# Expert rows rounded and split on VectorE before their transpose, which runs in the rounded format

## What is computed

```python
logits = jnp.einsum('th,eh->te', xf, gate_w)
expert_idx = jnp.argmax(logits, axis=-1)
onehot = jax.nn.one_hot(expert_idx, gate_w.shape[0], dtype=x.dtype)
g = jnp.einsum('th,ehd->etd', xf, wg)
u = jnp.einsum('th,ehd->etd', xf, wu)
inter = jnp.square(jax.nn.relu(g)) * u
inter = inter * onehot.T[:, :, None]
out = jnp.einsum('etd,edh->th', inter, wd)
...
g = _silu(_L0_ffn_ref(xn, ...))
x = x + s * g
```

## Time and profile before

| | us |
|---|---|
| median of 3 runs | 510.59 |
| lowest and highest | 508.68 and 511.1 |
| the profiled execution's own time | 510.11 |
| its span, first to last instruction | 508.2 |
| PE busy | 494.7 (97%) |
| DVE busy | 452.9 (89%) |
| ACT busy | 395.6 (78%) |
| POOL busy | 319.8 (63%) |

### The profile page before, as it was taken

One profiled execution on the slowest core, in us unless ns is written; L12 is line 12 of the kernel. 1 busy time (PEld: TensorE's weight loads), 2 busy tenths in 40 slices (PEclk: granted clock), 3 DMA queues, 4 the chain that ended last, 5 costly groups with the idle time before them and its releaser, 6 DMA issues.

```text
span 508.2 us, 11940 instructions
## 1 busy us (share of the span) xinstructions
PE 494.7 (97%) x3599; PEld 462.8 (91%) x3599; DVE 452.9 (89%) x1428; ACT 395.6 (78%) x910; POOL 319.8 (63%) x377
## 2 busy tenths in 40 slices
PE   6899999999999999999999999999999999999996
PEld 5899999999999999889999997898888888888885
DVE  6899999999999988969889948999999999999985
ACT  4878878787878784378988865888888888888885
POOL 5568876767676777454552027777887777877300
PEclk9999999999999999999999999999999999999999
DMA  7942322222222114457878563265665565665411
GB/s 224 254 115 94 113 86 94 85 84 84 84 84 84 43 52 142 175 159 245 249 242 261 184 199 113 74 144 130 137 151 126 129 140 126 144 142 127 103 43 64
DMA packets 59303, 67.70 MB, mean 133 GB/s; under 512 B 11880, under 2 KB 53616, under 8 KB 59248
## 3 DMA queue, kind: packets, MB, share of 16 engines
q1 hardware_dynamic: 44304, 38.69, 25.1%
q0 software_dynamic: 14944, 28.32, 22.3%
HBM read 39.85 MB, written 27.13 MB: 132 GB/s over the span
## 4 chain that ended last, share of the span: by engine, by line
PE 93%; DVE 3%; ACT 1%; issue 1%; DMA 1%; SPq 0%; DVEq 0%
PE q_ps L1524 11%; PE v_ps L1546 11%; PE gu_ps L1181 6%; PE s_ps L1566 6%; PE y_ps L1200 4%; PE k_ps L171 3%; PE m_ps L173 3%; PE m_ps L171 3%; PE k_ps L173 3%; PE m_ps L172 3%; PE k_ps L172 3%; PE t_ps L1157 3%; PE tq_ps L171 3%; PE tq_ps L172 3%; PE t_ps L1537 3%; PE tq_ps L173 3%
## 5 line engine op out<-in xcount | busy, mean ns | idle before, releaser
L1970 POOL DMA_INDIRECT four<-expert_rows,gather_u x64 | 68.5, 1071 | 37.2 <-DMA expert_rows<-y 18.5
L976 POOL DMA_INDIRECT sorted_rows<-xn,row_u x64 | 67.6, 1057 | 17.5 <-issue 14.3
L965 POOL TENSOR_TENSOR xn<-xn 128x512 fp32r<-128x512 f32 x32 | 43.2, 1350 | 30.5 <-ACT xn L581 30.4
L1524 PE MATMUL q_ps<-xt,wqk 128*128 128x256 f32 x256 | 60.6, 379 | 0.2 <-issue 0.2
L1546 PE MATMUL v_ps<-wvo,xt 128*128 128x256 f32 x248 | 58.7, 379 | 0.0
L1524 PEld LDWEIGHTS q_ps<-xt,wqk 128*128 128x128 f32 x256 | 48.5, 190 | 7.2 <-issue 0.7
L1546 PEld LDWEIGHTS v_ps<-wvo,xt 128*128 128x128 f32 x248 | 44.8, 190 | 4.8
L1976 POOL DMA_DIRECT2D res<-in_L_attn_x x26 | 34.9, 1341 | 18.7 <-DVE res L1773 17.1
L227 POOL DMA_DIRECT2D four<-sorted_rows x36 | 20.0, 555 | 39.9 <-PE t_ps L1157 35.0
L1985 POOL TENSOR_TENSOR rstd<-var_eps,neg_half 128x4 f32<-128x4 f32 x32 | 35.6, 1113 | 8.8 <-DVE var_eps L1809 8.7
L171 PE MATMUL tq_ps<-xt,wq 128*128 128x256 f32 x128 | 38.4, 300 | 1.7 <-DVE xt L715 1.7
(11 more groups left out here) (292 smaller groups left out, 1792.7 us busy)
## 6 DMA issues: line engine op xcount, KB each, us to landing
expert_rows<-y SPq DMA_DIRECT2D x35, 256.0 KB, 3.5
four<-in_L_attn_x SPq DMA_DIRECT2D x32, 256.0 KB
out_rows<-att SPq DMA_DIRECT2D x31, 256.0 KB
res<-in_L_attn_x POOLq DMA_DIRECT2D x26, 256.0 KB
four<-sorted_rows POOLq DMA_DIRECT2D x36, 128.0 KB, 3.4
four<-sorted_rows SPq DMA_DIRECT2D x36, 128.0 KB, 3.7
wdn<-in_L_ffn_wd SPq DMA_DIRECT2D x2, 512.0 KB, 7.2
sorted_rows<-res SPq DMA_DIRECT2D x8, 128.0 KB, 5.6
```

Of the source, the lines that this page charges most:

```text
L965: nc.gpsimd.tensor_tensor(xn2[:, s, 1], xn[:, i], xn2[:, s, 0].bitcast(F32), ALU.subtract).then_inc(g["xn_split"], 1)
L976: nc.gpsimd.indirect_dma_start(out=z.sorted_dram.ap(), out_offset=bass.IndirectOffsetOnAxis(ap=row_u[:, i // CU, k:k + 1], axis=0), in_=xn ...
L1524: m = nc.tensor.matmul(q_ps[:, j, :], wqk[:, k, j * P:(j + 1) * P], xt[:, i % 2, k, :], start=(j == 0 and k == 0), stop=(k == KD - 1), ski ...
L1970: nc.gpsimd.indirect_dma_start(out=moe[:, n % SLOTS, t, :], out_offset=None, in_=z.expert_dram.ap()[0:(z.SLOTS - 1) * P, :], in_offset=bas ...
```

## The change

`hidden` writes the product once, into a `hid` of 64 columns a tile, all in SBUF. Two new instructions on DVE follow in the same function: a copy of `hid` into the first half of `hid2` in the rounded format, and the difference `hid - rounded` into its second half. `turn_hidden` transposes `hid2` in fp32r, with an identity matrix in the same format (`ident_r`), which one new copy makes at the start of DVE's part of the stage. `copy_hidden` stays and now signals `ht_copied` itself; `hidden_rest` is gone. `gate_up` waits for the new semaphore `hid_made`, counted by the product, where it waited for `hid_ready`, now counted by the difference. The larger buffers move the space that the second layer keeps free from 3648 to 4032 numbers.

```diff
-        hid = sb("hid", [P, 2, 2, 2, DE])
+        hid = sb("hid", [P, 2, 2, DE])
+        hid2 = sb("hid2", [P, 2, 2, 2, DE], F32R)
+        ident_r = sb("ident_r", [P, P], F32R)
...
                 if reused:
-                    pe.wait_ge(g["hid_ready"], n - 1)
+                    pe.wait_ge(g["hid_made"], n - 1)
...
             def turn_hidden(n, i, reused):
+                if n == 0:
+                    pe.wait_ge(g["ident_rounded"], 1)
                 pe.wait_ge(g["hid_ready"], n + 1)
                 if reused:
                     pe.wait_ge(g["ht_copied"], n - 1)
                 for u in range(width(n)):
-                    t = nc.tensor.transpose(ht_ps[:, i % 2, u * P:(u + 1) * P], hid[:, i % 2, u].rearrange("p c f -> p (c f)"), z.ident[:])
+                    t = nc.tensor.transpose(ht_ps[:, i % 2, u * P:(u + 1) * P].bitcast(F32R), hid2[:, i % 2, u].rearrange("p c f -> p (c f)"), ident_r[:])
                 t.then_inc(g["ht_ready"], 1)
...
-                nc.scalar.activation(hidt[:, i % 2, 0:w], ht_ps[:, i % 2, 0:w * P].rearrange("p (u t) -> p u t", u=w), ACT.Copy).then_inc(g["ht_rounded"], 1)
+                nc.scalar.activation(hidt[:, i % 2, 0:w], ht_ps[:, i % 2, 0:w * P].rearrange("p (u t) -> p u t", u=w), ACT.Copy).then_inc(g["ht_copied"], 1)
...
-                twice = [P, w, 2, DE]
-                nc.vector.tensor_tensor(hid[:, i % 2, 0:w], o[:, :, DE:2 * DE].unsqueeze(2).to_broadcast(twice),
-                                        gate[:, i % 2, 0:w].unsqueeze(2).to_broadcast(twice), ALU.mult).then_inc(g["hid_ready"], 1)
-
-            def hidden_rest(n, i):
-                dve.wait_ge(g["ht_rounded"], n + 1)
-                w = width(n)
-                nc.vector.tensor_tensor(hidt[DE:P, i % 2, 0:w], ht_ps[DE:P, i % 2, 0:w * P].rearrange("p (u t) -> p u t", u=w),
-                                        hidt[DE:P, i % 2, 0:w], ALU.subtract).then_inc(g["ht_copied"], 1)
+                nc.vector.tensor_tensor(hid[:, i % 2, 0:w], o[:, :, DE:2 * DE], gate[:, i % 2, 0:w], ALU.mult).then_inc(g["hid_made"], 1)
+                dve.wait_ge(g["hid_made"], n + 1)
+                nc.vector.tensor_copy(hid2[:, i % 2, 0:w, 0], hid[:, i % 2, 0:w]).then_inc(g["hid_rounded"], 1)
+                dve.wait_ge(g["hid_rounded"], n + 1)
+                nc.vector.tensor_tensor(hid2[:, i % 2, 0:w, 1], hid[:, i % 2, 0:w], hid2[:, i % 2, 0:w, 0].bitcast(F32), ALU.subtract).then_inc(g["hid_ready"], 1)
...
-                if 1 <= m <= PAIRS:
-                    hidden_rest(m - 1, (m - 1) % QUAD)
...
+            nc.vector.tensor_copy(ident_r[:], z.ident[:]).then_inc(g["ident_rounded"], 1)
             divisors(START[0])
...
-    MOE_SPACE = 3648
+    MOE_SPACE = 4032
```

More of the change, by code:

```diff
@@ L1079, in experts @@
         y_banks = y_ps[:].rearrange("p i u d -> p i (u d)")
-        g = sems("weights_loaded shifts_ready shift_found t_ready t_copied gu_ready gate_relu squared hid_ready ht_ready ht_rounded ht_copied y_ready "
+        g = sems("weights_loaded shifts_ready shift_found t_ready t_copied gu_ready gate_relu squared hid_made hid_rounded hid_ready ht_ready ht_copied ident_rounded y_ready "
                  "y_tanh silu_ready wdn_rounded wdn_split w2_centred")
```

## The result

The changed kernel takes 515.87 us in the median of 4 runs (514.44 to 517.07), the kernel before 510.11 us beside it (4 runs, 508.68 to 511.1). The ratio is 1.0124, with an interval of 1.0103 to 1.0145: 1.2% slower. Forecast were 514.0 us and a range to 515.8. The direction was right, the loss was 5.8 us where 3.4 were expected, and the time lies just above the range.

What follows compares the result with a forecast made beforehand. PE, busy 97% of the span, was taken as the bound. Weights +2.9, split_end +1.2, removed waits -0.7 and transposes 0 gave +3.4 us on 510.11, or 513.5; with 0.5 for the median, 514.0 us, range 509.8 to 515.8.

Steps and rivals of the forecast that it cites:

- What bounds, and the chain: Expert steps: PE sets the pace at 2.03 us a step; DVE's new work of 1.77 us costs an undisturbed step nothing.
- What goes: PE's `down` no longer waits for `hidden_rest` where DVE was late, including the last steps: a gain of 0.7 us.
- -0.4: The sum in us that the forecast would end near without the rule that DVE and GpSimd share SBUF ports.
- DVE and GpSimd in SBUF: The new copy and difference, all operands in SBUF, stand still beside GpSimd's eleven operations: +2.9 and +1.2 us.
- turns: Rival at pair 1: SBUF access alternates between DVE and GpSimd, PE loads 1.6 us later, total 512.6 us; chance 22 in 100.
- no holding up: Rival: operations of 128 numbers are too short for the port lock to matter, 510.2 us, no change; chance 13 in 100.
- +2.9: Pair 1: three weight subtractions in a row hold the copy, PE loads 3.0 us later, less 0.1 of an old wait.
- split_end: Eight GpSimd operations, each starting with a step; four delay PE's load by 0.3 us each, +1.2 us in sum.
- the very first: The first of GpSimd's eight split_end operations, claimed to end when the copy comes, so given no cost.
- The transposes: 71 transposes of hidden rows change format to fp32r, claimed to stay at 0.11 us each: +0 us.
- Dear: Rival: the fp32r transposes of hidden rows take 0.22 us each, +7.8 us, total 521.8 us; chance 10 in 100.
- cheap transposes: Rival: the fp32r transposes of hidden rows take 0.06 us each, -3.5 us; chance 8 in 100, 2 more without holding up.

Runs made afterwards that it cites:

- e2: Changed kernel with GpSimd's three weight subtractions and eight split_end operations all held until behind DVE's copy and difference; 511.5 us, ratio 1.0007.
- e7: Changed kernel with the product written to PSUM and read there by copy and difference, GpSimd's operations left in place; 512.04 us, ratio 1.003.
- e6: Changed kernel with the rounded half written by a second product reading PSUM instead of the copy from SBUF; 515.84 us, ratio 1.0103.
- e3: Changed kernel with 25 unused identity transposes keeping PE busy ahead of the transpose of pair 1; 515.97 us, ratio 1.0101.
- e5: Kernel before the change, with DVE waiting ahead of pair 1's product until GpSimd's three weight subtractions end; 514.85 us, ratio 1.0084.
- e8: Changed kernel with only the eight split_end operations held behind the copy, the weight subtractions left at pair 1; 515.23 us, ratio 1.0096.
- e11: Kernel before the change, with the wait of e5 and the 25 unused transposes of e3; 512.37 us, ratio 1.0062.
- e1: Changed kernel with GpSimd's three weight subtractions moved apart, behind loads for pairs 8 to 10 and held until the difference; 514.34 us, ratio 1.005.
- e4: Changed kernel with its transposes of hidden rows in float32 again; 517.42 us, ratio 1.0113.
- e10: Kernel before the change, with the wait of e5 cut to two of GpSimd's three subtractions; 510.79 us, ratio 1.0031.
- e9: Changed kernel with GpSimd's three weight subtractions spread, each ahead of its loads for pairs 8, 9 and 10, without new waits; 513.81 us, ratio 1.0079.

## Why the prediction was right and wrong

**What bounds, and the chain.** Right. Away from collisions two steps take 4.0 to 4.1 us (pairs 22 to 32 of e2) against the forecast 2.03 each, so the longer chain on DVE costs nothing there. The copy of 128 numbers took 0.227 us (0.21 forecast). The price of a copy of 0.29 was too low: the text left it 0.15 us of cover and no cost, and e7, with such a copy, is 0.9 us longer over the stage.

**What goes.** 0.7 us of gain forecast, of which 0.3 were to be lost at pair 1. e2 is nowhere near -0.4: its stage is as long as before (-0.02). By the squaring of pair 17 it had gained 0.55; by pair 21 all but 0.1 was back, across PE's wait for the owners near 263 us: from the start of the last gate product to the next transpose are 0.65 us there and 0.37 in the kernel before. So the gain was made and then spent, most likely on that wait; no run took it apart. The prediction did not ask what is late next for this term.

**DVE and GpSimd in SBUF.** Right in mechanism and at pair 1 in size: a row of three operations holds one copy for 2.84 us, PE waits 2.77 where 3.0 were forecast, and *turns* (1.6) and *no holding up* fall. e6 and e7 show the cause, all operands in SBUF, apart from format and count. The engines do not meet at semaphores only, as the text on the chip has it: VectorE and GpSimd meet in SBUF too.

**The failed step.** It is the sentence "PE stands behind that wait with `down(0)`, the next transposes and gate products, so nothing fills it" with "+2.9" behind it: the wait was priced at its own length. An idle PE lost its clock too, and the pairs behind it ran at half the clock for some 6 us (0.50 from 227.4, when PE went on, to 233.7). Only rows at the low level could have priced that, and the kernel before had none in the stage; still the text should have asked what an idle stretch of nearly 3 us, the longest of the stage, does to an engine that is otherwise never idle. e3, e5, e8 and e11 show the term: 1.3 to 2.7 us, where the sum had nothing.

**The mis-sized term.** split_end: 4 x 0.3 = 1.2 us forecast, 2.4 measured (e1 less e2). The wait at the weight load was right (0.26 to 0.29), and so was the reading that three of the eight fall where PE loads the owners: those cost 0.2 us in sum. Two things were not. An open collision costs the pace more than its wait, 0.44 us in the mean. And the very first, at pair 7, was read from the old timeline as just over when the copy comes; in the new one it holds the copy for 0.70 us like the others, so five lie open and not four. 5 x 0.44 + 0.2 = 2.4.

**Luck in the number.** The median lies only 0.07 us above the range, but the stage is 7.45 us longer where 3.4 were forecast. What lies behind the stage was 1.15 us shorter in the profiled execution, and the upper bound had been set for slower transposes, which did not come.

**The transposes.** Right: the format costs nothing. From the first gate product of a step to `down`, with the two transposes between them, are 1.02 us with the rounded format (e2, from 281.30) and 1.03 with float32 (e4, from 280.67). *Dear* and *cheap transposes* fall.

## What to carry to other kernels

Before an operation of VectorE is moved from PSUM to SBUF operands, list GpSimd's tensor operations of that stage; a short operation waits for all of a row of them, and keeping one operand in PSUM, or letting GpSimd start behind it, removed the hold entirely here. Price a wait of the bounding TensorE at its length plus a second term: here 1.3 to 2.7 us of low clock behind 2.5 to 2.9 us of waiting, and about as much, in some executions only, behind 1.6. Where two engines share the rhythm of a loop, one collision comes again in every turn. Price it by what the next steps lose and not by its wait alone, and look for the collisions in the new timeline: one that is just missed in the old can be a full one there.

## What the hardware showed

- Behind a wait of PE of 1.63 us in an otherwise full program the granted clock went from 1.00 to 0.50 (e10, profiled), by times and mean clocks in 3 of 10 runs of the same kernel, which are 2.5 us slower; behind 1.87 us it stayed at 1.00 in the profiled run of e9. 25 transposes that nobody reads kept it at 1.00 through 3 us (e3, e11).
- GpSimd goes ahead of an operation of VectorE that began 0.36 us before it by the records (e9; the earlier trace rows has the same with 0.12 us). The Trainium skill gives the ports to the side that issues first ("SBUF — State Buffer", section "Who interferes with whom"); by the starts in this trace it was the other one. Either the start of a record is not where the access is claimed, or the rule does not hold here; no run tells them apart. Both cases have a transfer that GpSimd issues just ahead of its operation. Such a transfer without an operation behind it held nothing: in e2 over 20 copies and differences overlap one and keep their 0.23 and 0.29 us. What makes GpSimd's claim early is open.
- A held operation is not cheaper for being short: 0.23 us of work took 2.84.
- The hold seems to go the other way too: GpSimd's third subtraction took 1.66 instead of 1.28 us in e1 and in e2, where a 512-wide operation of VectorE with SBUF operands (0.68 us from 231.99) ran as it began:

```profile
231.99 0.68 DVE L1358 TENSOR_TENSOR shift_all<-chosen,moved 128x512 f32<-128x512 bf16 x1
...
232.15 1.66 POOL L1145 TENSOR_TENSOR w<-w,w_end 128x512 f32<-128x512 f32 x1 [0.21 <-DVE hid L1342]
```
